# Second attention: the global probabilities turned by 128x128 transposes in two halves, and both marks of the global queries loaded with the first group

## The reference, cut to what matters

```python
rel = k_idx[None, :] - q_idx[:, None]
local_ok = (rel <= 0) & (rel >= -(lw - 1))            # lw = 128
key_global = (k_idx % gs == 0)[None, :]               # gs = 64
query_is_global = (q_idx % gs == 0)[:, None]
allowed = (local_ok | key_global | query_is_global) & (rel <= 0)
scores = jnp.where(allowed, scores, jnp.float32(-1000000000.0))
w = jax.nn.softmax(scores, axis=-1)
out = jnp.einsum('bhtk,bhkd->bhtd', w, v)
```

## Time and profile before

| | us |
|---|---|
| median of 3 runs | 3097.73 (3094.49 to 3100.23) |
| the profiled execution: its time / its span | 3095.59 / 3093.9 |
| PE busy | 2944.3 (95% of the span) |
| DVE busy | 2622.5 (85%) |
| ACT busy | 1699.0 (55%) |
| POOL busy | 1270.7 (41%) |

### The profile page before, as it was taken

How to read it: one execution, slowest core, us unless ns; L and a number is a source line. 1 busy time by engine, 2 the same in 40 slices (tenths; PEclk the granted TensorE clock), 3 DMA queues, 4 the chain that set the end, 5 groups by cost and what they waited for, 6 DMA issues and landing times. The chain is left out here.

```text
span 3093.9 us, 105510 instructions
## 1 busy us (share of the span) xinstructions
PE 2944.3 (95%) x41228; PEld 2156.1 (70%) x41260; DVE 2622.5 (85%) x5413; ACT 1699.0 (55%) x3301; POOL 1270.7 (41%) x1570
## 2 busy tenths in 40 slices
PE   7999999999999899999996996999999979999998
PEld 4556777777777477777774654877777757777776
DVE  5778999999999599999994996777777679999997
ACT  5646887778787633333332773666565633333333
POOL 3561112112121244444441784565555644444442
PEclk9998999999999999999998997999999989999999
DMA  6682444444443222222222667555555332222221
GB/s 210 224 244 56 97 105 98 98 100 101 100 105 81 67 80 86 88 85 88 85 80 77 206 213 200 129 144 140 140 140 144 104 90 83 89 85 89 85 88 52
DMA packets 362151, 353.88 MB, mean 114 GB/s; under 512 B 79066, under 2 KB 298714, under 8 KB 361642
## 3 DMA queue, kind: packets, MB, share of 16 engines
q1 hardware_dynamic: 357162, 347.56, 41.2%
q10 hardware_dynamic: 4608, 0.79, 0.1%
HBM read 211.37 MB, written 135.27 MB: 112 GB/s over the span
## 5 line engine op out<-in xcount | busy, mean ns | idle before, releaser
L947 DVE TENSOR_REDUCE aA_nmax<-bank 128x1 f32<-128x512 f32 (+3 forms) x1216 | 714.6, 656 | 59.1 <-PE bank L1009 52.6
L991 ACT ACTIVATE aA_prob<-bank 128x512 f32<-128x512 f32 (+1 forms) x1216 | 617.5, 581 | 155.7 <-PE bank L1009 150.5
L1009 PE MATMUL bank<-aA_qk 96*32 96x512 bf16 (+17 forms) x12288 | 654.8, 317 | 15.8 <-issue 10.3
L1009 PEld LDWEIGHTS bank<-aA_qk 99*32 99x32 bf16 (+1 forms) x12288 | 407.8, 96 | 181.2 <-issue 51.4
L932 POOL TENSOR_SCALAR_AFFINE_SELECT aA_prob<-aA_prob 128x512 f32<-128x512 f32 x256 | 160.9, 634 | 666.9 <-ACT aA_prob L991 666.9
L1009 PE MATMUL bank<-aA_prob,aA_vq 128*32 128x512 f32 (+3 forms) x3072 | 356.3, 489 | 0.9 <-POOL aA_prob L932 0.9
L1499 PE MATMUL bank<-aB_qk 96*32 96x160 bf16 (+4 forms) x9344 | 311.9, 232 | 26.5 <-DVE aB_nfar L1378 15.0
L1499 PEld LDWEIGHTS bank<-aB_qk 96*32 96x32 bf16 (+3 forms) x9344 | 244.0, 99 | 110.4 <-issue 32.9
L1470 ACT ACTIVATE aB_prob<-bank 128x512 f32<-128x512 f32 (+1 forms) x512 | 262.4, 574 | 84.4 <-PE bank L1499 80.3
L1372 DVE TENSOR_REDUCE aB_nnear<-bank 128x3 f32<-128x480 f32 (+1 forms) x352 | 207.8, 636 | 55.2 <-PE bank L1499 50.4
L1353 POOL TENSOR_SCALAR_AFFINE_SELECT aB_prob<-aB_prob 128x512 f32<-128x512 f32 x256 | 163.4, 638 | 197.7 <-ACT aB_prob L1470 195.8
(11 more groups left out here) (211 smaller groups left out, 6288.7 us busy)
## 6 DMA issues: line engine op xcount, KB each, us to landing
aA_qk<-parts_A SPq DMA_DIRECT2D x384, 128.0 KB, 4.0
aB_qk<-parts_B SPq DMA_DIRECT2D x384, 128.0 KB, 3.3
parts_A<-pA_part SPq DMA_DIRECT2D x96, 256.0 KB, 4.8
parts_B<-pB_part SPq DMA_DIRECT2D x96, 256.0 KB, 3.0
o_A<-aA_o_sb SPq DMA_DIRECT2D x32, 512.0 KB, 2.9
o_B<-aB_o_sb SPq DMA_DIRECT2D x32, 512.0 KB, 2.9
pA_xin<-x SPq DMA_DIRECT2D x16, 512.0 KB, 4.5
v_A<-pA_vs SPq DMA_DIRECT2D x16, 512.0 KB, 4.6
```

Source lines behind the costliest of these rows:

```text
L947: nc.vector.tensor_reduce(dst, src, AX.X, ALU.max, negate=True).then_inc(s["m_taken"], 1)
L991: nc.scalar.activation(dst, src, ACT.Exp, scale=SCALE).then_inc(s["e_taken"], 1)
L1009: return nc.tensor.matmul(out, lhsT, rhs, start=start, stop=True, skip_group_check=True)
```

## The change

`gturn` becomes two units of four real transposes each. A transpose yields all 128 columns, so four fill a bank; ACT copies every second column of each bank, 256 of 512, to half of `pgT`. The planner's costs and due times are changed with it. On SP, the marks of both `qg` buffers are loaded with group 0, and none with group 1.

```diff
         for c in range(2):
-            unit("e", "gexp", c, 180, "act", 710, -0.7, ("dve", "gmax", n, 1), then=[("act", "gturn", pre, 0)])
-        unit("e", "gturn", 0, 1150, "act", 620, -0.55, ("act", "gexp", n, 1), then=[("pe", "og", pre, 0)])
-        unit("m", "og", 0, 1150, "dve", 500, -0.35, ("act", "gturn", n, 0), ("pool", "vq", n, 0),
+            unit("e", "gexp", c, 180, "act", 710, -0.7, ("dve", "gmax", n, 1), then=[("act", "gturn", pre, c)])
+        for c in range(2):
+            unit("e", "gturn", c, 550, "act", 400, -0.6, ("act", "gexp", n, c), then=[("pe", "og", pre, 0)])
+        unit("m", "og", 0, 1900, "dve", 500, -0.4, ("act", "gturn", n, 1), ("pool", "vq", n, 0),
...
-            sp.dma_start(qg[n][KROWS:K_GLOB, :, :],
-                         gfix_dram.rearrange("p (h i) -> p h i", h=HQ)).then_inc(s["gfix_loaded"], 16)
+            for p in range(2 if n == 0 else 0):
+                sp.dma_start(qg[p][KROWS:K_GLOB, :, :],
+                             gfix_dram.rearrange("p (h i) -> p h i", h=HQ)).then_inc(s["gfix_loaded"], 16)
...
-        def global_copy(n, _):
-            act.wait_ge(s["e_made"], after("e", "gturn", n, 0))
+        def global_copy(n, c):
+
+            act.wait_ge(s["e_made"], after("e", "gturn", n, c))
             if n >= 1:
                 act.wait_ge(s["m_made"], after("m", "og", n - 1, 0))
-            nc.scalar.activation(pgT[:, :, :, :].rearrange("p k h i -> p (k h i)"), bank_of("e", "gturn", n, 0),
-                                 ACT.Copy).then_inc(s["e_taken"], 1)
+            nc.scalar.activation(pgT[:, 4 * c:4 * c + 4, :, :].rearrange("p k h i -> p (k h i)"),
+                                 bank_of("e", "gturn", n, c)[:, ::2], ACT.Copy).then_inc(s["e_taken"], 1)
...
-        def global_turn(n, _):
-            pe.wait_ge(s["e_taken"], max(after("e", "gexp", n, 1), bank_clear("e", "gturn", n, 0)))
-            out = bank_of("e", "gturn", n, 0).rearrange("p (k i) -> p k i", k=QT)
-            for k in range(QT):
-                ins = mul(out[:, k, :], pg[:, k * P:(k + 1) * P], ident[:, ::2], True)
+        def global_turn(n, c):
+            pe.wait_ge(s["e_taken"], max(after("e", "gexp", n, c), bank_clear("e", "gturn", n, c)))
+            out = bank_of("e", "gturn", n, c).rearrange("p (k i) -> p k i", k=4)
+            for k in range(4):
+                ins = nc.tensor.transpose(out[:, k, :], pg[:, (4 * c + k) * P:(4 * c + k + 1) * P], ident[:, :])
             ins.then_inc(s["e_made"], 1)
...
-            pe.wait_ge(s["e_taken"], after("e", "gturn", n, 0))
+            pe.wait_ge(s["e_taken"], after("e", "gturn", n, 1))
             need(pe, s["m_taken"], bank_clear("m", "og", n, 0))
```

## The result

The changed kernel takes 3083.86 us (median of 5 runs, 3080.2 to 3085.93) against 3097.73 us (median of 5 runs, 3091.88 to 3100.23): ratio 0.9956, 95% interval [0.9945, 0.9968], 13.9 us or 0.44% faster. The forecast was 3068, a gain of 29.5 us. The time lies inside the range of 3059 to 3087, but less than half of the forecast gain came. The profiled execution of the changed kernel has a span of 3082.1 us, before it was 3093.9.

A forecast was written before the change was run, and what follows sets the result against it. The prediction took PE's instruction list to bound the inner stretch of attention B. Its terms, -31.5 (turn) + 2 (ring and list) + 0 (marks) + 0 (end) = -29.5 us, gave 3068 us from 3097.73, range 3059 to 3087.

The forecast's parts named there:

- The premise: Attention B, 1920 to 2460 us: the stage lasts as long as PE's list, so cuts there shorten it almost one to one.
- The turn on PE: Attention B's gturn: 8 transposes at 0.11 us replace a 1.93 us burst, saving 1.05 us a group, 31.5 in 30 groups.
- The longer ring: Line "e" in attention B: 22 uses of three banks a group instead of 21, plus a new planner list, costing 2 us.
- The copy on ACT: ACT's turn copy: two of 364 ns replace one of 597, +0.13 us a group, covered by ACT's slack, 0 on the span.
- The marks: At the seam PE starts 5.0 us sooner and gives it back waiting for group 2's queries and keys: 0.
- The end: Last group's turn: a shorter turn only lengthens the pause before the final exp units' rows land; 0, at best 1 us.
- Rival 1: DVE's full stretch and the new list turn half the saving into waits on nfar or near units: gain 16, 3082, 15%.
- Rival 2: The seam pays as well: exp pieces move ahead of far of group 2, 5.0 us stay won, time 3061, chance 10%.
- Rival 3: Slower: PE parks at the first half's transposes behind gexp; half-way 1.7 us a group, +20 us, time 3117, chance 7%.
- Rival 4: Transposes pace like the old matmuls, 0.12 us a record with two records each; no saving, time 3098 to 3100, 3%.
- The signs named beforehand: 256 gturn records near 0.11 us, PE busy some 33 us lower, groups near 16 us, PE at 97%, copy 364 ns, seam wait moved.

The follow-up runs named there:

- before_half: The kernel before with 4 of the turn's 8 matmuls left out from group 1 on, list unchanged: ratio to before 0.9971, -9.0 us.
- turn_double: The changed kernel with every transpose of the turn done twice, same list: ratio to the kernel before 1.0015.
- mm_halves: The changed kernel's list and two halves, each turned by four old 64-column matmuls and copied as 256 neighbours: ratio to the kernel before 1.0018, +5.6 us.
- exp_less_turn_half: The kernel before with a quarter of the window's exp strips and half the turn's matmuls left out from group 1 on: ratio 0.9911, -27.6 us.
- after_exp_less: The changed kernel without the last of four column strips in each window exp unit from group 1 on: 0.9913 of the kernel before, 3073.37 us.
- pad_waits: The kernel before with 36 more long-fulfilled wait instructions a group on PE, 1152 in all: ratio to before 1.0125, +38.7 us.
- exp_less_pad: The kernel before with the last exp strips cut and 36 fulfilled waits a group put in: ratio to before 1.0019, +5.9 us.
- only_new: The changed kernel without PE's attention B waits that an earlier wait on the same semaphore covers: 0.9909 of the kernel before, 3070.95 us.
- costs_only: The kernel before with its single turn and only the planner's new costs and due times: ratio to before 1.0045, +14 us.
- old_numbers: The changed kernel with the planner's numbers of before, halved for the two halves: ratio to the kernel before 0.9956.
- exp_less: The kernel before without the last of four column strips in each window exp unit from group 1 on: ratio to before 0.9998.
- one_mask: The changed kernel with each near-unit mask added by one matmul over 128 rows instead of four strips: ratio to the kernel before 1.0098, +30 us.

## Why the prediction was wrong

**The premise** failed: "What leaves that list shortens the span almost one to one, until DVE (75%) or the dependences between two engines take over." It was drawn from PE's 97.5% and the unbroken piece of the chain. On the unchanged list 27 us left and 9 came (before_half); on the changed one 18 of 27 came (turn_double) and 19 of 27.5 (mm_halves), each time against the changed kernel. What took over was neither DVE nor a dependence: in before_half PE's waits for `nfar` did not grow (8.7 us in 23 waits of 1945 to 2420 us, before 9.0 in 21), its "issue" waits did. The runs point to PE's own supply of instructions as the second bound: with the strips gone about 27 us came of the same cut (exp_less_turn_half) and of the change (after_exp_less). That it is the supply, and not the array work that goes with the strips, is argued from the stalls' tie to the packets and from the waits in pad_waits, exp_less_pad and only_new; it isn't shown by a run of its own. The rows were there: 12.2 us of PE's waits were "issue", which I read as what no other engine ends and then left aside as small. It is small in part because a record outlasts the distance to the next start and so covers the first 0.2 us or more of each gap. That it would grow when fast work takes the place of slow work was the question not asked. The Trainium skill warns of the first reading (page "Perfetto Trace Analysis", section "Identifying the Most-Contended Engine"): since matmuls are pipelined, the busy share of the matmuls is no good measure of how close PE is to its roofline. This case agrees: the inner stretch was at 97% before and after.

**The turn on PE** was mis-sized: 1.17 us a group and not 0.88, a saving of 23.3 us and not 31.5. A half takes 0.164 us for its first step, 0.109 for each of the next two, as in the bursts that the price came from, and 0.203 from its last transpose to what follows. The price of a transpose was right, then, and what was missing are the two ends of a burst, some 0.15 us a burst. The burst of before had the same ends (0.163 + 14 x 0.112 + 0.203 = 1.93), so the 1.93 held them once and my 0.88, taken from bursts behind whose last transpose matmuls with loads of 128 columns of f32 start at once, not at all: once for the place and once more for the break, 0.29 us a group. The step's own bound, 28.2 us, was too narrow: it priced the break alone, with one load. The estimate by the Trainium skill's load rule (page "TensorE: Matmul & The Clock Gate", section "LDWEIGHTS (loading the stationary operand)"), 25.7, came nearer, but not for the rule's sake: its 107 ns agree with the steps inside a burst here (0.109 for a transpose, 0.112 for a matmul of before; the load's own record is 0.140), and it leaves the ends out on both sides, 0.23 us of the old burst and 0.32 of the new ones.

**The longer ring** was taken at 2 us; mm_halves measures 5.6. By the distances between starts its turn takes 2.085 us a group instead of 1.942, 4.3 us in 30 groups, which is the second break and belongs to the term above; 1.3 are left for list and ring, within 3 us either way by the interval, so the 2 were near. The planner's numbers alone are worth +14 us with a single turn and nothing with two halves (costs_only, old_numbers), so the 2 were right by luck more than by reason: a new list has no price that rows of the old one show, and the bound of 9.7 would have been too low.

Put together: of the 15.6 us that are missing, 8.2 are the turn's size. The other 7.4 came back, and 5.7 more, when the strips were left out: 27.0 in after_exp_less, against 23.3 - 2 = 21.3 by the terms. The inner stretch holds next to none of the 5.7, for by its starts it is 21.9 us shorter; the interval of the whole begins at 22.6. So they lie at the ends of the stage or in the spread between executions, and no run tells which.

**The copy on ACT** was right: 385 ns, hidden behind ACT's waits for PE. **The marks** were right in size (-0.6 us measured alone) and in mechanism: PE starts `gmax` after POOL's copy, the `exp` pieces run 2.7 us sooner though the stage began 2.9 later, and the DMA of group 2's queries and keys ends the wait as before. The windows of PE (us, busy, PEclk, DMA share, GB/s) show the clock behind that wait, in the changed kernel and in one window of before that the earlier trace rows leave out:

```profile
1923.00:1926.00 3.00, 3.00 (x63) 0.50 0.80 160
1926.00:1929.00 3.00, 3.00 (x58) 0.78 0.86 186
1929.00:1932.00 3.00, 2.96 (x112) 1.00 0.81 178
```

```profile
1923.00:1926.00 3.00, 3.00 (x50) 0.63 0.88 185
```

The clock goes from its lower level, 1.2 GHz, to 2.4 GHz within the window of 1926 to 1929 us, and before within that of 1923 to 1926. The wait itself ends 2.7 us later than before (1922.54 against 1919.81), so the return moved by no more than the wait did: the longer wait cost no further clock. **The end** gave 1.3 us where 0, at best 1, was said: from the start of the last turn to the last `pv` burst (2463.78 to 2480.45 before, 2451.81 to 2467.18 after) 16.67 became 15.37.

**The rivals.** Rival 1 had the size (a gain of 16, time 3082) and the wrong cause: PE's waits for DVE's `nfar` did not grow (6.0 us in 15 waits against 9.7 in 23), and ACT's wait for `gneg` fell from 39.7 to 19.0 us (all waits of 1925 to 2460 us):

```profile
ACT aB_pg L1477 <- DVE aB_gneg L1419: 19.0, 10, 2.6
...
PEld bank L1502 <- DVE aB_nfar L1380: 6.0, 15, 0.6
PEld bank L1580 <- ACT aB_pgT L1485: 5.8, 14, 0.4
```

Its chance of 15% was right for a loss of half by anything; it should have been a rival of its own, "PE is full by another measure too". Rival 2 is excluded by the chain at 1917.09. Rival 3 leaves a trace of 5.8 us in 14 waits of the turn's weight loads for a `pgT` copy on ACT and 1.6 us in 6 for `aB_pg`, together 0.25 us a group and far below its 1.05. Rival 4 is excluded by the 256 records.

**The signs named beforehand.** PE's share above 95%, the number of records, the copy and the seam came as said, and still the time did not: these signs can't see a loss that PE's busy time covers. Three others told the truth. The records' mean spacing inside a half was 0.128 us and not 0.11, a group took 17.3 us and not 16, and PE's busy time over the span fell by 15.3 us (2944.3 to 2929.0), not 33.

## What to carry to other kernels

An engine that is busy 97% by its records may still wait: measure it by the distances between starts, and ask which supply ends each gap inside a run of equal instructions. Where PE runs many short matmuls, as here, array time and instruction count can bound it together, so a change that trades slow instructions for fast ones must be priced against both, and a cut of one alone (exp_less: nothing; before_half: a third) tells little about the two together. Price the ends of a burst apart from its steps. Count fulfilled waits as instructions, and leave out those that an earlier wait covers; but do not buy fewer instructions with matmuls that can't run side by side.

## What the runs showed of the hardware

- The packets of 16 KB on queue 8 (294 in the span before) follow the number of PE's instructions. The 1984 instructions fewer of exp_less made 7 packets fewer (287), the 1152 more of pad_waits 5 more (299): some 230 to 280 instructions a packet.
- In the changed kernel, before_half and before alike a packet comes every 4.66 us (102 in 475 us), though their groups take 17.32, 17.37 and 17.78 us; with the redundant waits out it is 4.57 (104, only_new), and in one_mask 5.46 (87), with no stall. With more waits it is 4.80 (99, pad_waits). So 4.66 us is neither a floor nor a fixed pace of the supply.
- A stall inside a unit (over 0.45 us, 1945 to 2420 us) ends 1.1 to 1.7 us after a packet has landed in 253 of the 261 cases in all 18 kernels; five of the other eight are in costs_only. In one_mask there was none.
- A fulfilled wait on PE costs 34 ns in the kernel before (pad_waits), 6 ns in the one without the strips (exp_less_pad: 6.5 us above exp_less for 1152), and gives back 37 and 39 ns when it is left out (14.6 us / 391 between changed kernel and only_new, 14.0 us / 360 on the kernel before).
- A burst of f32 transposes (128x128) or of the old turn's matmuls between strip matmuls takes 0.16 us for its first step, 0.109 or 0.112 for each one inside and 0.20 for the last; where f32 matmuls with loads of 128 columns follow, in projection B, the last takes 0.109 too.
